# The attention mask, moved from a matrix product into the tiles of the attention bias

## The reference, cut to what matters

```python
scores = jnp.einsum('bhqd,bhkd->bhqk', q / math.sqrt(HEAD_DIM), k)
scores = scores + attention_bias                  # 16 x 16 x 256 x 256
scores = jnp.where(src_mask, -jnp.inf, scores.astype(jnp.float32))
probs = jax.nn.softmax(scores, axis=-1).astype(v.dtype)
ctx = jnp.einsum('bhqk,bhkd->bhqd', probs, v)
```

## Time and profile before

| | |
|---|---|
| Median of 3 runs | 924.88 us (922.01 to 927.58) |
| The profiled execution: its time, its span | 921.48 us, 919.6 us |
| PE busy, share of the span | 812.3 us, 88% |
| DVE | 755.9 us, 82% |
| ACT | 621.0 us, 68% |
| POOL | 172.8 us, 19% |
| mean granted TensorE clock | 0.966 |
| DMA moved | 137.59 MB, 150 GB/s on the mean |

### The profile page before, as it was taken

How to read it: one execution, slowest core, us unless ns; L and a number is a source line. 1 busy time by engine, 2 the same in 40 slices (tenths; PEclk the granted TensorE clock), 3 DMA queues, 4 the chain that set the end, 5 groups by cost and what they waited for, 6 DMA issues and landing times.

```text
span 919.6 us, 18573 instructions
## 1 busy us (share of the span) xinstructions
PE 812.3 (88%) x5962; PEld 694.2 (75%) x5962; DVE 755.9 (82%) x2475; ACT 621.0 (68%) x1279; POOL 172.8 (19%) x160
## 2 busy tenths in 40 slices
PE   2276789999999999999999999999999999998782
PEld 0264668888889787888888888878888888787681
DVE  3648586798989989898989899898989898969565
ACT  1123668786868686877878686868788796777330
POOL 2100002121220403121212113030212121201110
PEclk9687899999999999999999999999999999999986
DMA  6714587667774757675686958486667657572100
GB/s 200 225 65 123 140 192 179 159 147 184 166 183 133 171 142 180 155 168 153 160 180 153 182 135 185 135 182 152 164 150 184 159 135 173 156 174 63 52 34 12
DMA packets 147737, 137.59 MB, mean 150 GB/s; under 512 B 19298, under 2 KB 144803, under 8 KB 147636
## 3 DMA queue, kind: packets, MB, share of 16 engines
q1 hardware_dynamic: 147636, 136.33, 60.6%
HBM read 98.49 MB, written 4.23 MB: 112 GB/s over the span
## 4 chain that ended last, share of the span: by engine, by line
PE 62%; ACT 18%; issue 8%; DVE 6%; SPq 4%; DMA 2%; POOL 1%; POOLq 0%; DVEq 0%; ACTq 0%
PE back_bank L1054 12%; PE turn_bank L1010 9%; PE context_bank L1064 6%; PE score_bank L1112 5%; PE front_bank L1048 5%; PE score_bank L1113 4%; ACT sc L529 4%; PE front_bank L1081 4%; ACT ffT L597 4%; PE back_bank L1034 3%; PE attend_bank L1034 3%; PE back_bank L1025 3%; PE front_bank L1218 2%; SPq L308 2%; ACT L529 2%
## 5 line engine op out<-in xcount | busy, mean ns | idle before, releaser
L529 ACT ACTIVATE sc<-sc,negmax 128x256 f32<-128x256 f32 x512 | 230.4, 500 | 39.0 <-DVE negmax L844 38.5
L844 DVE CUSTOM_DVE_ANT_0 sc<-score_bank,side 128x256 f32<-128x256 f32 x512 | 195.2, 419 | 37.9 <-PE score_bank L1113 34.1
L515 ACT ACTIVATE pt<-turn_bank 128x512 f32<-128x512 f32 x176 | 104.8, 595 | 134.7 <-PE turn_bank L1010 94.7
L1010 PE MATMUL turn_bank<-ident,sc 128*128 128x128 f32 x1024 | 157.2, 276 | 1.3 <-ACT sc L529 1.2
L1010 PEld LDWEIGHTS turn_bank<-ident,sc 128*128 128x128 f32 x1024 | 123.3, 141 | 32.3 <-issue 13.7
L452 POOL TENSOR_TENSOR rstd<-var,half_neg 128x2 f32<-128x2 f32 x64 | 54.3, 848 | 436.6 <-DVE var L773 435.3
L1112 PE MATMUL score_bank<-ks,qs 128*128 128x256 f32 x512 | 122.6, 321 | 8.0 <-DVE negmax L844 6.7
L1054 PE MATMUL back_bank<-w,ffT 128*128 128x256 f32 x512 | 118.0, 379 | 0.0
L1054 PEld LDWEIGHTS back_bank<-w,ffT 128*128 128x128 f32 x512 | 97.0, 190 | 12.7
L1113 PE MATMUL score_bank<-mask_neg,ident_r 128*128 128x512 f32 x256 | 102.1, 399 | 0.0
L1112 PEld LDWEIGHTS score_bank<-ks,qs 128*128 128x128 f32 x512 | 78.3, 192 | 16.7 <-DVE negmax L844 8.9
(11 more groups left out here) (209 smaller groups left out, 1990.0 us busy)
## 6 DMA issues: line engine op xcount, KB each, us to landing
side<-in_side SPq DMA_DIRECT2D x128, 512.0 KB, 5.1
qs<-qh SPq DMA_DIRECT2D x128, 64.0 KB, 4.2
ks<-kh SPq DMA_DIRECT2D x128, 64.0 KB, 3.8
ks<-kl SPq DMA_DIRECT2D x128, 64.0 KB, 4.3
qs<-ql SPq DMA_DIRECT2D x128, 64.0 KB, 4.4
wb<-in_wb SPq DMA_DIRECT2D x16, 512.0 KB, 6.7
xN<-in_x SPq DMA_DIRECT2D x16, 256.0 KB, 4.8
ada<-ada_rows SPq DMA_DIRECT2D x16, 256.0 KB, 4.9
```

The lines of the kernel that those rows point to most:

```text
L515: e.activation(pt[:, h % NP2, :, :], two(tbank[h % 2]), ACT.Copy).then_inc(copied[h % 4], 1)
L529: i = e.activation(sc[:, h % NS, q, :], sc[:, h % NS, q, :], ACT.Exp, bias=negmax[:, q, h:h + 1], scale=-1.0)
L844: i = e.tensor_tensor_reduce(sc[:, s % NS, q, :], two(sbank[s % 2])[:, q, :], side[:, (H * X.i + s) % NSIDE, q, :], -1.0, 3.4e38, ALU.add, ...
L1010: i = e.transpose(tbank[h % 2][:, k * S + q * P:k * S + q * P + P], sc[:, h % NS, q, k * P:k * P + P], ident[:, :])
```

## The change

The product with mask_neg goes, and so do mask_neg, ident_r and DVE's copy into ident_r. POOL now fills each pair of side rows with the mask times -2^127, 128 x 1024 elements in one instruction; it waits for that fill by its own semaphore and issues the load of the pair from its own queue with accumulation (accum_op add), so that the load adds the bias to what lies in the tile. The waits for the ring (heads 2c-1) move from SP to POOL with it. mask_raw has two buffers. The first three pairs are now filled and issued by POOL in slot 0 of t = -1, ahead of its step power(F, 1).

Three operations change their slots: x2b from slot 13 of B to slot 1 of the next t, after y_ready; x1res from slot 14 to slot 13, after xa_ready and ahead of power(G, 0); u_l from slot 1 to slot 0, ahead of the norm steps. ACT's copy of a turned head in slot 13 comes ahead of the feed-forward steps of that slot.

```diff
-SET0 = 2
+SET0 = 1
@@ tiles
-        mask_raw = sb("mask_raw", [P, TT, S // 4], I32)
-        mask_neg = sb("mask_neg", [P, 2, TT, S], F32R)
-        ident_r = sb("ident_r", [P, P], F32R)
+        mask_raw = sb("mask_raw", [P, 2, TT, S // 4], I32)
@@ sync
-            def load_side(x, c):
...
                     if s == 0 and F:
-                        wait(e, ev["mask_ready"], F.p)
-                        e.dma_start(mask_raw[:, :, :], d["mask"][bass.ds(F.i, 1)].rearrange("b (t p) n -> p (b t) n", p=P)).then_inc(ld_mask, 16)
-                        if t == -1:
-                            for c in range(3):
-                                load_side(F, c)
-                    if s % 2 == 0 and X and (s < 12 or F):
-
-                        c = s // 2
-                        head(e, biased, X, 2 * c - 1)
-                        if not (t == 0 and s == 0):
-                            load_side(X if c < NPAIR - 2 else F, (c + 2) % NPAIR)
+                        wait(e, ev["side_filled"], NPAIR * (F.i - 1))
+                        e.dma_start(mask_raw[:, F.par, :, :], d["mask"][bass.ds(F.i, 1)].rearrange("b (t p) n -> p (b t) n", p=P)).then_inc(ld_mask, 16)
@@ gpsimd
+            def load_side(x, c):
+
+
+                at = (H * x.i + 2 * c) % NSIDE
+                if c == 0:
+                    e.wait_ge(ld_mask, times(x, 16))
+                masked = mask_raw[:, x.par, :, :].bitcast(U8).unsqueeze(1).broadcast_to([P, 2, TT, S])
+                e.tensor_scalar(side[:, at:at + 2, :, :], masked, MASKED, None, ALU.mult).then_inc(ev["side_filled"], 1)
+                e.wait_ge(ev["side_filled"], NPAIR * x.i + c + 1)
+                e.dma_start(side[:, at:at + 2, :, :], d["side"][bass.ds(x.i, 1), 2 * c:2 * c + 2].rearrange("b h (t p) k -> p (b h) t k", p=P),
+                            accum_op=ALU.add).then_inc(ld_side[c], 16)
...
+                    if s == 0 and t == -1:
+                        for c in range(3):
+                            load_side(F, c)
+                    if s % 2 == 0 and X and (s < 12 or F):
+                        c = s // 2
+                        head(e, biased, X, 2 * c - 1)
+                        if not (t == 0 and s == 0):
+                            load_side(X if c < NPAIR - 2 else F, (c + 2) % NPAIR)
+                    if s == 1 and T:
+                        if F:
+                            e.wait_ge(ev["y_ready"], F.n)
+                        e.wait_ge(ev["n3_ready"], T.n)
+                        e.tensor_tensor(x2b[:, :, :], x2[:, :, :], rows(b2r[:, :]), ALU.add).then_inc(ev["x2b_ready"], 1)
                     if s == 1 and F:
                         power(F, 1, ev["y_var"], ev["y_rstd"])
...
-                    if s == 14 and F:
+                    if s == 13 and F:
+                        if G:
+                            e.wait_ge(ev["xa_ready"], G.n)
                         wait(e, ev["x2_ready"], F.i - 1)
                         e.wait_ge(ev["x1_ready"], F.n)
...
-                    if s == 6 and F:
-                        e.wait_ge(ld_mask, times(F, 16))
-                        e.tensor_scalar(mask_neg[:, F.par, :, :], mask_raw[:, :, :].bitcast(U8), MASKED, None, ALU.mult).then_inc(ev["mask_ready"], 1)
...
-                    if s == 13 and B:
-                        e.wait_ge(ev["n3_ready"], B.n)
-                        if G:
-                            e.wait_ge(ev["xa_ready"], G.n)
-                        e.tensor_tensor(x2b[:, :, :], x2[:, :, :], rows(b2r[:, :]), ALU.add).then_inc(ev["x2b_ready"], 1)
@@ scalar
+                    if s == 13 and X:
+                        copy_turned(X, s - LT)
                     if s in (11, 12, 13, 14) and B:
...
-                        if s in ACT_COPIES:
+                        if s in ACT_COPIES and s != 13:
@@ vector
-            e.tensor_copy(ident_r[:, :], ident[:, :]).then_inc(ready, 1)
...
+                    if s == 0 and U:
+                        e.wait_ge(ev["uh_ready"], U.n)
+                        e.tensor_tensor(u_l[:, :, :], t_u[:, :, :], u_h[:, :, :].bitcast(F32), ALU.subtract).then_inc(ev["ul_ready"], 1)
...
-                    if s == 1 and U:
-                        e.wait_ge(ev["uh_ready"], U.n)
-                        e.tensor_tensor(u_l[:, :, :], t_u[:, :, :], u_h[:, :, :].bitcast(F32), ALU.subtract).then_inc(ev["ul_ready"], 1)
@@ tensor
-                        if s == 0:
-                            e.wait_ge(ev["mask_ready"], X.n)
                         for q in range(TT):
-                            e.matmul(two(sbank[s % 2])[:, q, :], qs[:, s // 2, q * P:q * P + P], ks[:, s, :], start=(q == 0), stop=False)
-                        i = e.matmul(sbank[s % 2][:, :], ident_r[:, :], mask_neg[:, X.par, :, :], start=False, stop=True)
+                            i = e.matmul(two(sbank[s % 2])[:, q, :], qs[:, s // 2, q * P:q * P + P], ks[:, s, :], start=(q == 0), stop=(q == TT - 1))
                         i.then_inc(scored[s % 4], 1)
```

More of the change, by code:

```diff
@@ L54 @@
 y_stats y_aggr y_var y_rstd x1_scaled x1_ready x1_turned x1T_ready
-q_done qh_ready ql_ready k_done kh_ready kl_ready mask_ready
+q_done qh_ready ql_ready k_done kh_ready kl_ready side_filled
 v_done v_ready x1res_ready ct_lo ct_hi nan_ready
@@ L356, in _ @@
             e.wait_ge(st_ada, 16)
-            def load_side(x, c):
-                e.dma_start(side[:, (H * x.i + 2 * c) % NSIDE:(H * x.i + 2 * c) % NSIDE + 2, :, :],
-                            d["side"][bass.ds(x.i, 1), 2 * c:2 * c + 2].rearrange("b h (t p) k -> p (b h) t k", p=P)
-                            ).then_inc(ld_side[c], 16)
             def stack(x, prev, m, blocks):
```

## The result

The changed kernel takes 1033.61 us (median of 4 runs, 1029.75 to 1036.16) against 924.75 us of the kernel before on the same chip: 1.117 times as long, with a 95% interval of 1.112 to 1.122. The forecast was 905 us and a range up to 1000; the result lies outside it, on the slow side. Its profiled execution spans 1027.9 us, 108 us more than before: the first nanz comes 19 us later, and 90 us lie between the first and the last.

What follows compares the result with a forecast made beforehand. It took PE to set the 50.2 us period, DVE 3 us behind; DVE's sum gave 47.8, 2.4 saved. 15 x -2.4 = -36, +16 at the start: 901.5 profiled, 905 as median; own range 885 to 920, whole range 882 to 1000.

Steps and rivals of the forecast that it cites:

- port conflicts: POOL's eight fills a sample holding DVE's two-input operations, 0.84 us each: 2.0 us a sample, bounds 0 and 6.7.
- Does the side row come in time: Tightest pair of side rows (heads 6, 7): in time by 1 us at the old pace, late by 0.5 at the new.
- PE's terms: PE loses 3.7 us (mask products), 1.2 (u_l) and 0.3 (ACT's copy) a sample: 50.2 to 45.0 us.
- The 1.2 and 0.3 us: PE's gaps in slots 2 and 14, to go by moving u_l to slot 0 and ACT's slot 13 copy earlier.
- DVE needs 44.2: DVE's work a sample, 45.3 less 1.1 us; with 2.0 of fill holds and 2.0 of waits, 48.2, counted as 47.8.
- x1res: Moved to slot 13 beside the one-input statistics, it no longer stalls DVE's L939: -1.1 us a sample.
- POOL: Fills 2.8, wait 0.1, issue 1.3 us per pair; 44.1 us a sample in all, under 47.8, some 90% busy.
- Rival (1): POOL becomes the bound if its issue g passes 1.9 us: 997 us at 2.5, near 1110 at 3.4; chance 0.34.
- Rival (2): Each fill holds DVE for its whole length, 11 us instead of 2, period 57.2: about 1045 us; chance 0.07.
- The start: Slot 0 of t = -1: POOL waits for the mask and does three fills before power(F,1): +16 us, bounds +13 and +22.

Runs made afterwards that it cites:

- the two kernels with the ring of eight: Side ring of eight heads instead of six: changed kernel with fills 1034.82 us; kernel with 40 semaphore increments in place of each fill, mask left out, 931.10 us.
- the delay of a fill alone: Changed kernel, mask left out, 40 semaphore increments on POOL (2.85 us) in place of each fill and its wait, accumulating loads kept: 982.14 us, 1.063.
- the kernel without fills: Changed kernel, mask left out, with no fill, wait or accumulation; POOL issues plain loads and all moves stay: 901.58 us, 0.975 of before.

## Why the prediction was wrong

**The step that failed is the one on port conflicts.** It put 2.0 us a sample for the fills' holds, between bounds of 0 and 6.7. Measured are 6.1 us a sample of longer DVE operations, some 4.7 of them the fills' own by the estimate above and the rest power's and bcf's, and 7 us of period between the two kernels with the ring of eight. The price of one hit on a two-input operation, 0.84 us, was right. Three things were off. The first is the number of hits: I took half a hold per hit and few hits, but an order written out by hand repeats every sample, and POOL met the same seven groups in nearly every sample. TENSOR_SCALARs had no entry, and they are held late in a fill; turning three of them into two-input operations gave 28.6 us back. And POOL's older steps moved with its fuller queue: bcf now holds L966, and a fill behind a power makes one hold out of two (438.38, 2.71 us). The sum had no term for them.

**"Does the side row come in time"** answered in time by 1 us, or late by 0.5. Landing (6.5 against 6 taken), issue (1.34 against 1.3) and fill were right, and yet the delay of a fill alone costs some 50 us with a ring of six. With eight that kernel takes 931 us, as much as the one without the delay and a ring of six (929). The slack was read at one pair of heads, at the pace of before; the other pairs stand behind rstd and x2b in POOL's queue, and I did not work them out. In the changed kernel this loss lies under the first: take most of the holds away, and it shows (1019 us with three memsets and two-input operations).

**PE's terms.** The 3.7 us of the mask products were worth nothing: the kernel without fills stays at 47.5 us a sample, the moves with mask products at 47.6. DVE's chain is as long there, and x3c's hold of t_e makes it so by 1 us a sample; what the 3.7 us bring without that hold no run shows. The 1.2 and 0.3 us (u_l, ACT's copy) brought nothing alone, where x3c holds the norm, and 8 us, 0.5 a sample, on top of the POOL moves. These holds by x3c are the failed step once more: the prediction looked for conflicts of the fills and of x1res only. That DVE needs 44.2 and some 2 of waits was near; that the period is then set by DVE, so that each hold comes in full, stood in the sum and would have been a reason to put the weight on its upper bound.

**x1res**: -1.1 a sample was right in kind; in the kernel with the moves alone L939 falls by 183 ns, four a sample, 0.7 us. The moves of x1res and x2b together bring 15.6 of the 24 us; no run separates them. In the changed kernel it is given back: L942's mean is 847 ns, as a fill now holds one of four.

**POOL** was right in that its sum stays under the period and in the issue (1.34 against 1.3); the wait is 0.3 (0.1 taken), and its busy share 65% instead of some 90, part of it for the longer period. Rival (1), g over 1.9 us, had 0.34 and did not come. Rival (2), a fill holding DVE for its whole length, gave 1045 us and 0.07; the measured 1034 is near its number by luck, for it came by another route: a hold of 0.84 us at the start of a fill and a second one for TENSOR_SCALARs at its end. The Trainium skill (SBUF — State Buffer, Who interferes with whom) would have a two-input instruction blocked for the whole fill; the trace denies that here, and agrees for the add of two tiles (1.26 us, held to its end).

**The start**, +16 us: the first norm came at 53.16 where 53.6 was said, and mending it gave 14.5 us. The first nanz came 19 us later.

By parts, in the order in which the kernels were built up: moves -24 us (900.1); mask products gone, POOL issues +1 (901.6); accumulation +28 (929.3); the delay of 2.85 us on POOL, start included, +53 (982.1); a fill in its place +51 (1033.6). The last two overlap: with a ring of eight the fill in place of the delay costs 104 us. What the delay costs with a ring of eight is not shown, for no kernel with that ring and without the delay was run.

## What to carry to other kernels

Count port conflicts by walking the other engine's written-out order once, operation by operation, for each comes back in every period; and walk all of its steps, the old ones too, since new work moves them. A hold on an engine close behind the bound counts in full. Work taken off the bounding engine is worth only the distance to the next one, here nothing (901.6 against 900.1 us): first build the kernel in which the new work costs nothing, for it bounds the gain in that order of steps. And when a change bundles moves with an idea, time the moves alone.

## What the runs showed of the hardware that was not expected

- A fill by POOL from one-byte input (128x1024, 2.77 us) holds DVE in two places: the first 0.77 to 0.9 us for two-input operations and TENSOR_SCALARs, and a late part for TENSOR_SCALARs alone (not for every one: L879 at 1.5 us is held, nanz at 1.5 us is not).
- A memset, which only writes, holds a TENSOR_SCALAR to its end (2.74 us beside 2.66) and no two-input operation (0.69).
- POOL's issue of an accumulating load of 512 rows of 1 KB takes 1.32 us, of a plain one 0.78, and holds no two-input operation of DVE (0.68 us inside it). A TENSOR_SCALAR was seen only 0.13 us ahead of one, and is free (0.43).
- The accumulating loads move their 67.1 MB in 67584 packets, the plain ones in 18432.
- A DMA of 64 bytes issued by POOL between accumulating loads is back only after some 6 us.
